# Keys and values of a typed graph layer in one table of 2 KB rows: one gather in eight fetches both, and its values stay in SBUF for the weighted sum

## The reference, cut to what matters

```python
k = typed_linear(x, node_type, Wk, bk).reshape(n, h, dk)      # n = 3125, h = 8 heads, dk = 32
q = typed_linear(x, node_type, Wq, bq).reshape(n, h, dk)
v = typed_linear(x, node_type, Wv, bv).reshape(n, h, dk)
k_r = jnp.einsum('nhd,rhde->rnhe', k, rel_att)                 # a key row per relation (8) and node
v_r = jnp.einsum('nhd,rhde->rnhe', v, rel_msg)                 # a value row per relation and node
key_e = k_r[etype, src]
val_e = v_r[etype, src]
att = (q[dst] * key_e).sum(-1) * rel_pri[etype] / sqrt_dk
seg = dst * r + etype                                          # softmax over the edges of a (dst, type)
alpha = ex / den[seg]
hmsg = jax.ops.segment_sum(alpha[..., None] * val_e, seg, num_segments=s)
```

## Time and profile before

| | us |
|---|---|
| median of 3 runs | 8556.6 (8552.79 to 8558.91) |
| the profiled execution | 8561.61 |
| its span, first to last instruction | 8559.7 |
| first to last gather of keys (scores) | 1766.6 to 2367.0 |
| first to last gather of values (sum) | 2582.5 to 3210.8 |
| VectorE busy, whole span | 3598.2 (42%) |
| GpSimd busy, whole span | 3435.4 (40%) |
| TensorE busy, whole span | 6177.8 (72%) |

### The profile page before, as it was taken

One profiled execution on the slowest core, in us unless ns is written; L12 is line 12 of the kernel. 1 busy time (PEld: TensorE's weight loads), 2 busy tenths in 40 slices (PEclk: granted clock), 3 DMA queues, 4 the chain that ended last, 5 costly groups with the idle time before them and its releaser, 6 DMA issues. The chain is left out here.

```text
span 8559.7 us, 87812 instructions
## 1 busy us (share of the span) xinstructions
PE 6177.8 (72%) x21499; PEld 3748.1 (44%) x21507; DVE 3598.2 (42%) x8884; ACT 1407.1 (16%) x2363; POOL 3435.4 (40%) x4286
## 2 busy tenths in 40 slices
PE   6668658457725667496464699999999999555645
PEld 1123224234412333485121466666666666443545
DVE  6822961156666665111995322222212222333622
ACT  0011001011110001121341122222222222111011
POOL 0766867756606770673773472000000000265022
PEclk9778889766756668798786799999999999555568
DMA  2022002123302330464002211111111111000045
GB/s 96 2 67 71 0 20 78 49 71 90 90 7 81 86 86 8 139 195 142 2 1 98 65 54 51 48 52 46 50 50 54 45 56 54 7 7 6 0 126 174
DMA packets 420073, 519.09 MB, mean 61 GB/s; under 512 B 174610, under 2 KB 341016, under 8 KB 419864
## 3 DMA queue, kind: packets, MB, share of 16 engines
q1 hardware_dynamic: 304024, 376.73, 14.0%
q0 software_dynamic: 115840, 139.64, 6.6%
HBM read 389.40 MB, written 126.18 MB: 60 GB/s over the span
## 5 line engine op out<-in xcount | busy, mean ns | idle before, releaser
L911 POOL COPY gs_from_ids<-gat_src_row 128x8 uint16 (+1 forms) x80 | 15.9, 199 | 2188.7 <-SPq L129 2188.4
L2221 PE MATMUL gg_p_all<-gg_edges,nodes 128*128 128x384 f32 (+2 forms) x2700 | 797.1, 455 | 0.6 <-DVE nodes L2368 0.6
L2221 PE MATMUL gg_p_all<-gg_edges,gg_other 128*128 128x384 f32 (+2 forms) x2700 | 797.3, 455 | 0.0
L2379 DVE SCALAR_TENSOR_TENSOR gg_gates<-gg_into,gg_per_edge,gg_p_all 128x384 f32<-128x384 uint16 (+2 forms) x216 | 124.3, 575 | 1343.1 <-PE gg_p_all L2244 1343.1
L2221 PEld LDWEIGHTS gg_p_all<-gg_edges,nodes 128*128 128x128 f32 x2700 | 502.3, 190 | 287.1 <-issue 1.0
L2221 PEld LDWEIGHTS gg_p_all<-gg_edges,gg_other 128*128 128x128 f32 x2700 | 502.4, 190 | 285.9
L1302 PE MATMUL ha_p_sum<-ha_weighted,ha_hot 128*128 128x258 f32 x832 | 389.8, 631 | 253.9 <-DVE sums L1263 243.0
L399 POOL DMA_INDIRECT cell_sorted<-cell_scatter_what,cell_scatter_at x392 | 437.3, 1116 | 170.2 <-issue 87.4
L2057 PE MATMUL ce_p_cell<-ce_hot_at,ce_hot_src 128*128 128x512 f16 (+1 forms) x1280 | 283.3, 354 | 295.3 <-DVE ce_hot_src L2017 143.9
L916 POOL DMA_INDIRECT ha_values<-v_table,ha_value_rows x416 | 407.4, 979 | 182.9 <-issue 93.5
L916 POOL DMA_INDIRECT hs_keys<-k_table,hs_key_rows x416 | 396.9, 954 | 183.1 <-issue 89.7
(11 more groups left out here) (502 smaller groups left out, 10844.0 us busy)
## 6 DMA issues: line engine op xcount, KB each, us to landing
gg_packed<-cell_counts SPq DMA_DIRECT2D x150, 800.0 KB, 4.3
e_w<-in_L_ffn_W_dram SPq DMA_DIRECT2D x64, 1024.0 KB
e_w<-in_L_ffn_W_dram SPq DMA_DIRECT2D x56, 512.0 KB
k_table<-hp_kr SPq DMA_DIRECT2D x25, 1024.0 KB
v_table<-hp_kr SPq DMA_DIRECT2D x25, 1024.0 KB
cell_counts<-cell_acc SPq DMA_DIRECT2D x5, 4000.0 KB
slots<-clear_zeros SPq DMA_DIRECT2D x15, 1024.0 KB
e_rows<-slots SPq DMA_DIRECT2D x60, 256.0 KB, 4.9
```

Of the source, the lines that this page charges most:

```text
L2221: mm = pe.matmul(p_all[:, half, 0:n], rows[:, t, half * P:(half + 1) * P], edges[:, turn % 2, t, 0:n], start=t == 0, stop=t == tiles - 1)
L2379: dve.scalar_tensor_tensor(out=to, in0=into[:, own], scalar=per_edge[:, i * halves + k:i * halves + k + 1], in1=p_all[:, bank, 0:n], op0=A ...
```

## The change

The two tables become one, `kv_table`, of rows of 512 numbers (2 KB): the key of a (type, node) first, its value behind it. Seen as rows of 1 KB the same memory has the key in row 2r and the value in row 2r + 1. `derive_edges` makes two lists of row numbers: `key_row` is 2r, and r itself in the last column of each eight; `src_row` becomes 2r + 1. In the scores seven gathers of eight fetch 1 KB key rows as before and the eighth fetches rows of 2 KB, key and value, into slot 7 and a new slot 8. VectorE copies the value part to `kept` (13,312 float32 a partition, 52 KB), after the product of that chunk and before the sum of the chunk ahead of it, and GpSimd's second half waits for that copy (`moved`) and no longer for the product. In the sum GpSimd issues seven gathers in each turn, and the eighth chunk's product reads `kept`.

The projection's weights lie in `kept` while it is not in use, the softmax's `temp` is `att`'s own memory, `q` is released before the softmax, and `values` has seven slots. The second graph of the kernel uses the same softmax; nothing else of it changes.

```diff
@@ derive_edges
-            ch.step(dve.scalar_tensor_tensor(out=e.table_row[:, :], in0=t0[:, :], scalar=float(g.tiles * P),
+            ch.step(dve.scalar_tensor_tensor(out=t0[:, :], in0=t0[:, :], scalar=float(g.tiles * P),
                                              in1=e.src_row[:, :], op0=ALU.mult, op1=ALU.add))
+            ch.inc(dve.tensor_scalar(e.key_row[:, :], t0[:, :], 2.0, None, ALU.mult))
+            ch.step(dve.tensor_scalar(e.src_row[:, :], t0[:, :], 2.0, 1.0, ALU.mult, ALU.add))
+            ch.step(dve.tensor_scalar(e.key_row[:, SLOTS - 1:n:SLOTS], t0[:, SLOTS - 1:n:SLOTS], 1.0, None, ALU.mult))
@@ hgt_project, SP
-            for n, table in enumerate((k_table, v_table)):
-                sp.dma_start(table.rearrange("(r n) d -> n r d", r=rels)[bass.ds(t * P + since * P, P), :, :],
-                             kr[:, n, :, :]).then_inc(s["kv_stored"], 16)
+            for n in range(2):
+                sp.dma_start(kv_table.rearrange("(r n) d -> n r d", r=rels)[
+                    bass.ds(t * P + since * P, P), :, n * dim:(n + 1) * dim], kr[:, n, :, :]).then_inc(
+                        s["kv_stored"], 16)
@@ hgt_scores
-    keys = ctx.enter_context(nc.sbuf_tensor("hs_keys", [P, SLOTS, g.dim], F32))
+    keys = ctx.enter_context(nc.sbuf_tensor("hs_keys", [P, SLOTS + 1, g.dim], F32))
-        led(pool, loops, gather_rows(pool, g, e.chunks, [(e.table_row, key_rows, k_table, keys, got)], staged, used))
+        by_key = kv_table.rearrange("n (k d) -> (n k) d", k=2)
+
+        def body(i, first):
+            for h in range(2):
+                half = slice(h * HALF, (h + 1) * HALF)
+                if not first:
+                    gate(pool, g, moved if h else used, i if h else i * SLOTS - HALF)
+                pool.tensor_copy(key_rows[:, half].bitcast(U16),
+                                 e.key_row[:, bass.ds(i * SLOTS + h * HALF, HALF)].bitcast(U16)).then_inc(staged, 1)
+                gate(pool, g, staged, i * 2 + (h + 1))
+                for b in range(h * HALF, (h + 1) * HALF):
+                    both = b == SLOTS - 1
+                    pool.indirect_dma_start(
+                        out=keys[:, b:b + 2, :].rearrange("p k d -> p (k d)") if both else keys[:, b, :],
+                        out_offset=None, in_=kv_table if both else by_key,
+                        in_offset=bass.IndirectOffsetOnAxis(ap=key_rows[:, b:b + 1], axis=0)).then_inc(got[b], 16)
@@ hgt_scores, VectorE, after the product of chunk b
+                if b == SLOTS - 1:
+                    dve.tensor_scalar(kept[:, bass.ds(i, 1), :], keys[:, SLOTS:SLOTS + 1, :], 1.0, None,
+                                      ALU.mult).then_inc(moved, 1)
@@ hgt_sum, GpSimd: as in the scores, from src_row, with used as the gate of both halves
+                for b in range(h * HALF, min((h + 1) * HALF, SLOTS - 1)):
+                    pool.indirect_dma_start(
+                        out=values[:, b, :], out_offset=None, in_=by_value,
+                        in_offset=bass.IndirectOffsetOnAxis(ap=value_rows[:, b:b + 1], axis=0)).then_inc(got[b], 16)
@@ hgt_sum, VectorE
-                    dve.wait_ge(got[b], i * 16 + 16)
+                    if b < SLOTS - 1:
+                        dve.wait_ge(got[b], i * 16 + 16)
+                    of = values[:, b, :] if b < SLOTS - 1 else kept[:, bass.ds(i, 1), :].rearrange("p o d -> p (o d)")
```

More of the change, by code:

```diff
@@ L987, in hgt_scores @@
 @phase
-def hgt_scores(g, e, q, k_table, att):
+def hgt_scores(g, e, q, kv_table, att, kept):
     nc = g.nc
@@ L1073, in segment_softmax @@
     scan = sb("scan", [P, length])
-    temp = sb("temp", [P, length])
+    temp = att[:, :, :].rearrange("p c h -> p (c h)")
     stage = sb("stage", [P, 3, P])
@@ L1222, in hgt_sum @@
 @phase
-def hgt_sum(g, e, v_table, att, sums, degree):
+def hgt_sum(g, e, kv_table, att, kept, sums, degree):
     nc = g.nc
@@ L2738, in build_rest @@
         y = scoped(own, "y0", node_shape)
-        q = scoped(own, "q", node_shape)
         edge_memory(g, hgt, own)
+        att = scoped(own, "att0", [P, hgt.chunks, heads])
+        kept = scoped(own, "kept", [P, hgt.chunks // SLOTS, g.dim])
+        asking = ExitStack()
+        q = scoped(asking, "q", node_shape)
         with together(g):
```

43 lines of the change are left out of this document (28 added, 15 removed).

## The result

The changed kernel took 8490.1 us (median of four runs, 8488.6 to 8498.1) against 8556.3 us for the kernel before (median of four, 8552.8 to 8558.9): a ratio of 0.9923, 95% interval 0.9908 to 0.9939. The profiled execution took 8490.6 us.

The account below looks back on a forecast made before the run. GpSimd's instruction stream was taken to bound scores and sum, VectorE close behind in the sum. Sum -51, long gathers 0, landing +0.4, copies +5, derivation +1.5: -44 us, from 8556.6 to 8513 us; 8-in-10 range 8494 to 8546.

Parts of the forecast that it names:

- VectorE's 11.07 us is late next: I take 11.10 us: Sum: with a gather gone, VectorE's chain with TensorE sets the turn at 11.10 us, down from 12.08; 51 us saved.
- its own arithmetic, written one sentence earlier as 10.83: Sum: GpSimd's instruction stream with one gather fewer takes 12.08 - 1.25 = 10.83 us a turn.
- Sum, 52 gathers fewer: Sum: one of eight gathers goes, 1.25 us of GpSimd a turn; 51 us saved, ends 26 and 93 us.
- the slots cover the uneven halves: Sum: GpSimd's halves of four and three gathers, 6.0 and 4.8 us, even out through the slots, with 3 us of room.
- The prediction's other end, 10.29: Sum: GpSimd's turn falls to 10.29 us if stretched copies and gathers vanish; 93 us saved if VectorE's chain is quicker too.
- Scores, the long gather: Scores: one gather in eight with 2 KB rows costs GpSimd nothing; bounds nothing and 65 us.
- The later landing: Scores: a 2 KB row lands after 3.2 us, not 2.8; VectorE's slack covers it, 0.4 us once at the stage's end.
- The copy: Scores: 52 VectorE copies to `kept`, 0.29 us each, hold GpSimd up by 0.1 us each, 5 us in all.
- Its upper bound: Scores: most the copies could cost by holding up GpSimd, 0.38 x 52 = 20 us.
- Derivation: Edge derivation: two more whole-width operations and one of 52 columns, covered by nothing; 1.5 us.
- The first rival: Sum: TensorE speeds up, VectorE's turn is 10.44 us and GpSimd's 10.83 decides; 65 us saved, 8499 us; chance 0.12.
- GpSimd should show waits for VectorE's products that it has not now: Sum: sign expected in the changed kernel's trace, with VectorE's wait for gathered values nearly gone.

Follow-up runs that it names:

- six gathers: Changed kernel, chunk 3 of each eight in the sum also reading `kept` instead of being gathered (wrong values): 8643.7 us against 8781.3 for the kernel before, 0.9843.
- no gathers: Changed kernel with GpSimd idle in the sum and all eight products reading `kept` (wrong values): 8632.2 us, 0.9834 of the kernel before.
- the small matmuls: Unused bf16 matmuls added per half of the sum: eight in the kernel before, at two places, 0.9997 and 0.9999; six in the kernel whose sum gathers nothing, 0.9806.
- moving the register loads: Kernel before, VectorE's register loads for the sum's adds moved ahead of the products: 8562.6 us against 8562.2, 1.0002; with eight added matmuls a half, 8557.4 us, 0.9994.

## Why the prediction was wrong

*Where it failed.* The step is "VectorE's 11.07 us is late next: I take 11.10 us". It read the runner-up's own time as the turn less its recorded wait, 12.08 - 1.01. Measured with the bound taken away it is 9.51 us. So nothing was late behind GpSimd, and its own arithmetic, written one sentence earlier as 10.83, decided: 10.79. 0.31 us a turn too much, 52 times, is 16 us of the 27 by which the profiled execution was missed (44 forecast, 71.0 measured). The others are the copies (5), the layernorm stage (5) and the derivation (0.6).

*Why turn less wait is not a floor.* In each kernel I took the halves one by one, from one-hot to one-hot in order of time, and summed their waits (mean us of a half; "rest" is execution, overlaps taken off, and what stands ahead of the one-hot; "slow" are halves with 1.0 us or more of waits for TensorE):

| kernel | halves | length | values | TensorE | issue | own result | rest | slow |
|---|---|---|---|---|---|---|---|---|
| before | 87 | 6.09 | 0.52 | 1.12 | 0.28 | 0.22 | 3.95 | 66 |
| changed | 88 | 5.43 | 0.17 | 0.98 | 0.17 | 0.22 | 3.89 | 52 |
| six gathers | 86 | 4.84 | 0.00 | 0.72 | 0.06 | 0.30 | 3.76 | 26 |
| no gathers | 87 | 4.78 | 0.00 | 0.81 | 0.00 | 0.22 | 3.75 | 28 |

Without its wait for values, a half before is 5.57 us, against 4.78 with no gathers: 0.79 a half, 1.58 a turn. It is made of 0.62 for TensorE, 0.56 of issue and 0.40 of rest. The issue and the rest come with a value that lands at the last moment: in the earlier trace rows the fourth product runs apart from the other three, and the first add begins 0.24 us after it. All 76 halves before that have a recorded wait for a value have this issue time ahead of the adds, and so have 10 of the 11 that have none, whose last gathered product begins 0.14 to 0.17 us after a landing; without gathers no half has it. In the half at 2807.78 above, four products take 1.42 us in one run and the add overlaps the last.

The clock is the lesser part. Before, 52 of 87 halves run at the low level (a granted clock near 0.50), and without gathers 26 of 87. Without gathers such a half takes 5.23 us and another 4.58; before, less the wait for values, it is 5.74 and 5.32. The change of the mix is then worth (52 - 26)/87 x 2 x 0.42 to 0.65 = 0.25 to 0.39 us a turn, an estimate, in line with the small matmuls. At the same level of the clock a half of the kernel before is still 0.5 to 0.7 us longer, 1.0 to 1.5 a turn. GpSimd's work beside it is not what does that: with six gathers and no wait for values, halves take 5.28 and 4.56 us at the two levels. So the recorded wait, 1.04 us a turn, was half or less of what goes with arriving late. That the waits exist beside each other is shown; that each of them would vanish by itself is not, and moving the register loads showed the opposite. How what is left beside the clock splits between VectorE and TensorE stays open.

*Sum, 52 gathers fewer.* The price of a gather, 1.25 us a turn, was right (1.29 with seven, 1.19 for the next). That the slots cover the uneven halves was right: GpSimd's halves take 6.04 and 4.78 us, as written down (6.0 and 4.8), while VectorE's take 5.40 and 5.45, and the gathers' span fell by 67 us and not by 26. The prediction's other end, 10.29 if stretched gathers vanish, did not come; they average 1016 ns now (979 before) and 1052 with six, and 45 of 364 now begin during a one-hot where 8 of 416 did.

*Scores, the long gather.* Right: GpSimd pays nothing, as the earlier trace rows said, and nothing with eight of them. The later landing was right too: the product of chunk 7 begins 3.37 us after its gather's start where it was 2.80 (medians of 52), and the last DMA packet of the long gather ends at 3.03 us, of the others at 2.44. VectorE's waits for that chunk grew from 12.3 to 38.9 us in the stage, and its slack covered them: the stage is 0.7 us longer. Such a gather and its product:

```profile
2010.36 0.95 POOL L1024 DMA_INDIRECT hs_keys<-kv_table,hs_key_rows  x1 [0.30 <-issue]
...
2013.80 0.42 DVE L1041 TENSOR_TENSOR hs_prod<-hs_keys,hq_p_rows 128x256 f32<-128x256 f32 x1 [0.48 <-DMA hs_keys<-kv_table,hs_key_rows]
```

*The copy.* 286 ns in the median, as read between the earlier trace rows. The 5 us for a hold-up of GpSimd was too much; eight times as many show none. Its upper bound called 0.38 us the copy's full length, which the same paragraph has at 0.29. The row it was taken from, is the one-hot's, which does stretch gathers and staging copies; the copy doesn't. The Trainium skill, "SBUF — State Buffer", section "Who interferes with whom", says that of a one-source copy in the two-port mode and a GpSimd instruction the one that issues first shuts the other out, and that an operation with two SBUF inputs contends only with what GpSimd reads. Here 416 such copies left every gather under 1.06 us, so GpSimd was not shut out, while copies that start 0.5 to 0.7 us into a gather took 455 ns for 286. The trace agrees with the rule in part: VectorE is the one that waits, but the 33 copies that start 0.3 to 0.5 us into a gather, and so come ahead of that stretch, hold up neither themselves (286 ns) nor the gather (956 ns). The prediction had taken the rule for a cost of GpSimd alone. The one-hot and the product, which have two SBUF inputs, took gathers that begin beside them from 0.95 to 1.38 us and more. That may be the page's own case, as the gather reads its offsets from SBUF; no run here tells that.

*Derivation.* 0.9 us instead of 1.5.

*The first rival* came nearest: 8499 us, "its turn would be 10.44 us and GpSimd's 10.83 would decide". The bound was right and its reason partly: VectorE waits less for TensorE in the denser loop (0.98 us a half instead of 1.12), but that is 0.14 of the 0.31 us by which a half less its wait for values got shorter (5.57 to 5.26). Its 10.44 us was no floor either. I had spoken against it that TensorE's work a turn is unchanged; it is the idle time between that changed. The rest down to 8490 is about what the copies, at nothing instead of 5 us, and the layernorm stage, 5 us shorter, make. "GpSimd should show waits for VectorE's products that it has not now" was the test named in the prediction, and the trace answered no.

## What to carry to other kernels

A turn less the recorded wait of the runner-up is an upper bound of the runner-up's own time, not its floor: data that lands late also breaks the overlap of what follows and goes with slower engines behind it. Take the runner-up's time from a stretch in which it never waits, or measure it with the bound's work taken out; if neither fills the turn, the bound goes on alone. Where an engine pays by the instruction and not by the byte, wider rows are free to it: eight gathers of twice the length cost GpSimd nothing here at a DMA share of 0.56. What a longer landing costs is up to the slack of who waits for it.

## What the runs showed of the hardware

An indirect gather of 128 rows costs GpSimd 0.95 us plus 0.30, from rows of 80 bytes to rows of 2 KB; its data is there 0.6 us later with rows of 2 KB than with rows of 1 KB. VectorE's operations with two SBUF inputs stretch a gather that begins beside them: from 0.95 to 1.07 us in the mean beside the 128x256 product and to 1.20 beside the 128x512 one-hot, 1.49 at most. A one-input copy doesn't stretch the gather; it is stretched itself, from 0.29 to 0.46 us in the mean, if it starts 0.5 to 0.7 us after the gather. TensorE's granted clock moves between 0.50 and nearly full speed from one half, or a few, to the next, and a half's length follows it.

In the sessions with the slower kernel before, the scores stage stands still again and again: each trace of the slowest two has 18 to 30 stretches of over 3 us from one gather's end to the next one's start, where the traces of the result have none. The transfers are not late there: by the DMA packets the last one of a gather ends 2.44 us after its start in the median, in either session. VectorE's waits from 1800 to 2360 are put down to TensorE's query rows and no longer to keys, in the changed kernel run again (first row) and in the result's run (the two others):

```profile
DVE hs_prod L1041 <- PE hq_p_rows L981: 160.5, 140, 3.2
```

```profile
DVE hs_prod L1041 <- DMA hs_keys<-kv_table,hs_key_rows: 135.1, 243, 2.0
DVE hs_prod L1041 <- PE hq_p_rows L981: 45.1, 102, 1.1
```

The sum's gathers, from the same table, show no such stretches. What makes that stage stand still was not found.
